# Attention and routed experts on one core: queries and keys projected with channels on the partitions, expert choice and first loads moved ahead, zeros written in the attention stage

## The reference

```
xn = layernorm(x)                       # x: 16 x 1024 x 256, float32
q, k, v = xn @ W_q, xn @ W_k, xn @ W_v  # split into 16 heads of 16 channels
q, k = rope(q), rope(k)                 # x * cos + [-x2, x1] * sin over each head's 16 channels
attn = softmax(causal(q @ k.T) / sqrt(16))
s = concat(attn @ v) @ W_o
logits = xn @ w_router.T                # 8 experts; every token goes to its argmax
h = leaky(xn @ w_fc[e].T, 0.5) ** 2     # only the chosen expert's output is kept
out = x + s * silu(h @ w_proj[e].T)
```

## Time and profile before

| | |
|---|---|
| median of 3 runs | 2603.72 us (2599.06 to 2605.83) |
| the profiled execution | 2609.07 us, its span 2607.3 us |
| PE, DVE, ACT, POOL busy, share of the span | 95%, 81%, 68%, 38% |
| project_phase | up to 428.7 us |
| attention_phase | 428.7 to about 2240 us |
| expert_output_phase | the rest |

### The profile page before, as it was taken

How to read it: one execution, slowest core, us unless ns; L and a number is a source line. 1 busy time by engine, 2 the same in 40 slices (tenths; PEclk the granted TensorE clock), 3 DMA queues, 4 the chain that set the end, 5 groups by cost and what they waited for, 6 DMA issues and landing times. The chain is left out here.

```text
span 2607.3 us, 53565 instructions
## 1 busy us (share of the span) xinstructions
PE 2484.7 (95%) x16876; PEld 1292.0 (50%) x16877; DVE 2110.2 (81%) x6183; ACT 1773.4 (68%) x4187; POOL 987.6 (38%) x1187
## 2 busy tenths in 40 slices
PE   7999993999999999999999999999999999899887
PEld 6888782334334334343343343343343343588776
DVE  7888886888889888899899888898888898355344
ACT  5777771577777777777777777777777777655211
POOL 7888885122222222222222222222222222222666
PEclk9999996899999999999999999999999999999898
DMA  7999997655646546546557556466465461498898
GB/s 241 356 346 355 353 340 205 124 93 106 116 99 109 113 91 114 116 93 117 103 99 150 104 101 118 93 104 118 99 108 115 91 110 48 139 308 303 271 349 258
DMA packets 305865, 435.04 MB, mean 167 GB/s; under 512 B 101808, under 2 KB 204464, under 8 KB 305584
## 3 DMA queue, kind: packets, MB, share of 16 engines
q1 hardware_dynamic: 293296, 398.05, 61.0%
q0 software_dynamic: 12288, 33.57, 4.7%
HBM read 241.18 MB, written 188.74 MB: 165 GB/s over the span
## 5 line engine op out<-in xcount | busy, mean ns | idle before, releaser
L866 ACT ACTIVATE probs<-ps_cols 128x512 f32<-128x512 f32 (+3 forms) x3072 | 1313.5, 498 | 478.9 <-PE ps_cols L1035 467.2
L887 DVE CUSTOM_DVE_ANT_0 dump<-ps_rows,mask 128x128 bf16<-128x128 f32 (+7 forms) x2048 | 1472.0, 754 | 199.2 <-issue 166.9
L1035 PE MATMUL ps_cols<-q_st,k_st 99*128 99x512 bf16 (+3 forms) x3072 | 857.6, 329 | 5.5 <-DMA q_st<-max_T 3.2
L845 POOL TENSOR_SCALAR_AFFINE_SELECT probs<-probs 128x512 f32<-128x512 f32 x512 | 324.6, 634 | 1321.3 <-ACT probs L866 1321.3
L979 PE MATMUL ps_rows<-k_st,q_st 96*128 96x512 bf16 (+3 forms) x3072 | 768.8, 330 | 27.2 <-DMA v_st<-v_dram 21.9
L1011 PE MATMUL ps_ctx<-probs,v_st 128*32 128x512 f32 (+3 forms) x6144 | 642.0, 497 | 1.6 <-ACT ctx_raw L858 0.8
L1035 PEld LDWEIGHTS ps_cols<-q_st,k_st 99*128 99x128 bf16 x3072 | 273.4, 97 | 595.0 <-ACT probs L866 390.1
L979 PEld LDWEIGHTS ps_rows<-k_st,q_st 96*128 96x128 bf16 x3072 | 277.5, 98 | 292.4 <-DVE row_max L887 130.4
L1011 PEld LDWEIGHTS ps_ctx<-probs,v_st 128*32 128x32 f32 x6144 | 129.3, 108 | 188.7 <-issue 113.5
L280 POOL TENSOR_TENSOR roped<-rope_c,rope_s 128x512 f32<-128x512 f32 x128 | 164.8, 1287 | 40.7 <-DVE rope_s L404 40.7
L887 DVE DVE_READ_ACCUMULATOR2_ANT row_max<- 128x1 f32 x2048 | 170.0, 83 | 0.2
(11 more groups left out here) (113 smaller groups left out, 2613.3 us busy)
## 6 DMA issues: line engine op xcount, KB each, us to landing
parts_dram<-parts SPq DMA_DIRECT2D x128, 384.0 KB, 3.9
q_st<-parts_dram SPq DMA_DIRECT2D x384, 128.0 KB, 4.4
k_st<-parts_dram SPq DMA_DIRECT2D x384, 128.0 KB, 6.9
v_dram<-v_sb SPq DMA_DIRECT2D x128, 256.0 KB, 5.5
v_st<-v_dram SPq DMA_DIRECT2D x64, 512.0 KB, 9.0
xs_dram<-zeros SPq DMA_DIRECT2D x36, 512.0 KB, 6.9
xs_sb<-xs_dram SPq DMA_DIRECT2D x72, 256.0 KB, 4.8
g_dram<-g_sb SPq DMA_DIRECT2D x72, 256.0 KB, 3.9
```

The costliest lines, as they stand in the source:

```text
L845: nc.gpsimd.affine_select(out=tri, in_=tri, compare_op=ALU.is_ge, fill=0.0, base=0, pattern=[[0, GH], [1, P]], channel_multiplier=-1).then ...
L866: nc.scalar.activation(probs[:, k % PB, h, 0:w], ps_cols[(GH * k + h) % CB][:, 0:w], ACT.Exp).then_inc(exp_done, 1)
L887: nc.vector.tensor_tensor_reduce(out=dump[:, even, 0:n], in0=ps_rows[:, 512 * bank:512 * bank + n], in1=mask[:, S - n:S], scale=1.0, scala ...
L1035: nc.tensor.matmul(ps_cols[(GH * k + h) % CB][:, 0:w], k_st[r][:, j // IB, h * 512 + (j % IB) * P:h * 512 + (j % IB + 1) * P], q_st[r][:, ...
```

## The change

- **Queries and keys are projected with channels on the partitions.** The weights are now the stationary operand and the turned tile the moving one (`heads` on PE). A unit `m` is one of 64: queries (`a` = 0) or keys (`a` = 1) of one tile. Its two banks hold the first and second half of every head's channels (`k` = 0, 1), so the swap of halves is a swap of banks. DVE makes four products of 128x512 per unit (`rotate`; for queries with the factor 1/4 in the same instruction), POOL combines them in two instructions of 128x512 (`turn`), and the result is already laid out as it is stored: PE's turn back is gone. The parts are cut per unit, 1024 columns at once, and `take_rest` reads `roped` in SBUF where it read `ps_m` in PSUM.
- **Normalisation half a tile sooner.** ACT applies the first two sub-tiles of tile `t + 2` at the end of tile `t`; DVE's statistics stand in one piece at the start of a tile.
- **Values** are stored in rows of 68 columns where they had 128: the heads lie 17 apart, and a head's matmul in attention still takes 32 columns, of which 17 are used.
- **Experts are chosen** (`choose`) after DVE's last `rotate` and before its last `take_rest`. The one-hot table is written in the order in which it lies in memory.
- **Constants** of the attention stage (mask, identities) are made in the first stage, whose start they follow; the first group's operands are loaded in tile 8 (`first_operands`, `load_operands`).
- **Zeros** are written in the attention stage, four pieces in each of the first nine groups; the 128 scatters follow in the other 55 groups, two or three each.

The diff, cut to its core:

```diff
+def load_operands(sp, parts_dram, v_dram, b, r, q, k, v, loaded):
+
+    for a, (dst, slots) in enumerate(((q, SLOT_Q), (k, SLOT_K))):
+        for slot, part in enumerate(slots):
+            src = parts_dram[:, a, part].rearrange("(b c) (d g h) t -> b g d c (h t)", c=TPB, g=NG, h=GH)[b, r]
+            sp.dma_start(dst[slot * HD:(slot + 1) * HD], src).then_inc(loaded, 16)
+    src = v_dram[:, r].rearrange("(b c) p n -> b p c n", c=TPB)[b]
+    sp.dma_start(v[:, 0:NB * V_ROW].rearrange("p (c n) -> p c n", c=TPB), src).then_inc(loaded, 16)
...
-            for i in range(CLEARS * t // NT, CLEARS * (t + 1) // NT):
-                clear_xs(i)
+            if t > 0:
+                store_parts(t - 1)
+            if t == FIRST_GROUP_AT:
+                for j in range(TPB):
+                    sp.wait_ge(v_stored[j % 2], 16 * (j // 2 + 1))
+                    sp.wait_ge(parts_stored[j % 2], 32 * (j // 2 + 1))
+                load_operands(sp, parts_dram, v_dram, 0, 0, *first_in)
             sp.wait_ge(v_ready, SUB * (t + 1))
-            for g in range(NG):
-                sp.dma_start(v_dram[t, g], v_sb[:, u, g]).then_inc(v_stored[u], 16)
-            sp.wait_ge(part3_done, SUB * (t + 1))
-            for blk in range(4):
-                sp.dma_start(parts_dram[t, blk].rearrange("a r t -> r a t"),
-                             parts[:, u, blk]).then_inc(parts_stored[u], 16)
+            sp.dma_start(v_dram[t].rearrange("g p n -> p g n"),
+                         v_sb[:, u].rearrange("p g s n -> p g (s n)")).then_inc(v_stored[u], 16)
+        store_parts(NT - 1)
         for u in range(2):
-            sp.wait_ge(v_stored[u], 16 * NG * NT // 2)
-            sp.wait_ge(parts_stored[u], 64 * NT // 2)
+            sp.wait_ge(v_stored[u], 16 * NT // 2)
+            sp.wait_ge(parts_stored[u], 32 * NT // 2)
             sp.wait_ge(xn_stored[u], 16 * NT // 2)
-        sp.wait_ge(xs_cleared, 16 * CLEARS)
...
+        def turn(m):
+
+            u = m % 2
+            pool.wait_ge(half_turned, m + 1)
+            if m >= 2:
+                pool.wait_ge(rest_ready, m - 1)
+            nc.gpsimd.tensor_tensor(roped[:, u, 0], rope_c[:, u, 0], rope_s[:, u, 0],
+                                    ALU.subtract).then_inc(roped_ready, 1)
+            pool.wait_ge(qk_used, 2 * m + 2)
+            nc.gpsimd.tensor_tensor(roped[:, u, 1], rope_c[:, u, 1], rope_s[:, u, 1],
+                                    ALU.add).then_inc(roped_ready, 1)
+
+        def part3(m):
+            t, a = divmod(m, 2)
+            pool.wait_ge(part2_done, m + 1)
+            nc.gpsimd.tensor_tensor(parts[:, t % 2, a, 2], rest[:, m % 2], parts[:, t % 2, a, 1],
                                     ALU.subtract).then_inc(part3_done, 1)
...
+        for m in range(NM + 2):
+            if m < NM:
+                turn(m)
+                if m % 2 == 0 and m // 2 + 2 < NT:
+                    scale(m // 2 + 2)
+            if m >= 2:
+                part3(m - 2)
...
+        def rotate(m):
+
+            t, a = divmod(m, 2)
+            u, at = m % 2, (t % TPB) * TOK
+            cos, sin = (rope_sb[:, i, at:at + TOK] for i in range(2))
+            first, second = ps_qk[2 * u], ps_qk[2 * u + 1]
+
+            def times(out, ps, table):
+                if a == 0:
+                    return nc.vector.scalar_tensor_tensor(out, ps[:], SCALE, table, ALU.mult, ALU.mult)
+                return nc.vector.tensor_tensor(out, ps[:], table, ALU.mult)
+
+            if m >= 2:
+                dve.wait_ge(roped_ready, 2 * (m - 1))
+            dve.wait_ge(qk_ready, 2 * m + 1)
+            times(rope_c[:, u, 0], first, cos)
+            times(rope_s[:, u, 1], first, sin).then_inc(qk_used, 1)
+            dve.wait_ge(qk_ready, 2 * m + 2)
+            times(rope_s[:, u, 0], second, sin).then_inc(half_turned, 1)
+            times(rope_c[:, u, 1], second, cos).then_inc(qk_used, 1)
+
+        def take_rest(m):
+            t, a = divmod(m, 2)
+            dve.wait_ge(part1_done, m + 1)
+            if m >= 2:
+                dve.wait_ge(part3_done, m - 1)
+            nc.vector.tensor_tensor(rest[:, m % 2], roped[:, m % 2].rearrange("p k t -> p (k t)"),
+                                    parts[:, t % 2, a, 0], ALU.subtract).then_inc(rest_ready, 1)
...
+        for m in range(NM + 1):
+            t, a = divmod(m, 2)
+            if m < NM:
+                if a == 0 and t + 2 < NT:
+                    ln_stats(t + 2)
+                    ln_scale(t + 2)
+                if a == 1 and t + 1 < NT:
                     xT_lo(t + 1)
...
+                rotate(m)
+            else:
+                choose()
+            if m >= 1:
+                take_rest(m - 1)
...
+        def heads(m, k):
+
+            t, a = divmod(m, 2)
+            cols = slice((2 * a + k) * P, (2 * a + k + 1) * P)
+            if m >= 2:
+                pe.wait_ge(qk_used, 2 * (m - 2) + k + 1)
+            three_passes(ps_qk[2 * (m % 2) + k][:], lambda i, c: w_all_hl[i][:, c, cols],
+                         lambda j, c: xT_hl[j][:, t % 2, c, :]).then_inc(qk_ready, 1)
...
+        for m in range(NM):
+            t, a = divmod(m, 2)
+            pe.wait_ge(xT_lo_ready, DC * (t + 1))
+            values(2 * m)
+            if a == 1 and t + 1 < NT:
+                transpose_xn(t + 1, (2, 3))
+            heads(m, 0)
+            values(2 * m + 1)
+            if a == 0 and t + 1 < NT:
+                transpose_xn(t + 1, (0, 1))
+            heads(m, 1)
...
-    SUBS_SCATTERED = NT * SUB // N
+    CLEARS = NBLK * BLK // (4 * P)
+    CLEAR_GROUPS = 9
+    CLEARED = CLEARS // CLEAR_GROUPS
+
+    def subs_scattered(n):
+
+        at = [NT * SUB * max(m - CLEAR_GROUPS, 0) // (N - CLEAR_GROUPS) for m in (n, n + 1)]
+        return range(*at)
...
+            if n < CLEAR_GROUPS:
+                for i in range(CLEARED // 2):
+                    clear_xs(CLEARED * n + i)
             store_ctx(n, b, r, 0)
             if not last:
                 load_max(n + 1, (r + 1) % RING, 0)
-            t = n // SUBS_SCATTERED + 1
-            if n % SUBS_SCATTERED == 0 and 2 <= t < NT:
-                sp.wait_ge(scattered[t % 2], 16 * SUB * (t // 2))
...
-                mm = nc.tensor.matmul(ps_ctx[VW * h:VW * (h + 1), o:o + w], v_st[r][:, j, VW * h:VW * (h + 1)],
+                mm = nc.tensor.matmul(ps_ctx[VW * h:VW * (h + 1), o:o + w], v_st[r][:, j * V_ROW + VP * h:j * V_ROW + VP * h + VW],
...
```

438 lines of the change are left out of this document (200 added, 238 removed).

## The result

| | before | after |
|---|---|---|
| median | 2602.52 us (2599.06 to 2605.83) | 2651.22 us (2650.50 to 2662.60) |
| profiled execution, its span | 2609.07, 2607.3 us | 2651.32, 2649.6 us |
| forecast for the median | | 2613, range 2564 to 2640 |

A forecast was written before the change was run, and what follows sets the result against it. The prediction took DMA to set the old tile period, PE half a microsecond behind. Its terms, 21.5 + 1 + 1.5 + 0 - 15.2 + 0.5, gave +9.3 us: 2613 us for the median, range 2564 to 2640.

The forecast's parts named there:

- tiles and the load in them: First stage: tile period 12.95 instead of 12.17 us, +21.5 us in all; loading group 0 in tile 8, +1.5.
- start: Before the tiles: weights cut in five instructions instead of one, on ACT and then DVE, 0 to 2 us, +1 taken.
- end of the stage: After the tiles: cheaper choice of experts against waits for POOL, 24.0 us against 24.3, counted as nothing.
- wait for group 0: Between first stage and row items: PE's wait while SP loads group 0's operands goes, -15.2 us.
- attention, first column scores to first expert block: Attention: zero pieces and a third scatter stay hidden behind PE, +0.5 us (0 to 3).
- the plain sums: Tiles: busy time per engine without exclusion, largest 10.3 us on POOL, giving a period of about 11.2 us.
- The price of 1.05 us on POOL: Tiles: what POOL pays for each subtraction when DVE is first, between 0 and 1.22 us, 1.05 taken.
- the barrier: Between first stage and attention: PE's first row item was to come within 1 us of it.
- the three rivals: Tiles: periods 11.2, 12.1 or 13.75 us, times 2554, 2585 or 2639; chances 0.16, 0.13, 0.16 (last with the clock).
- the gap: Tiles: once per tile POOL waits for DVE's statistics and three products, 0.2 to 0.6 us, 0.5 taken.
- the third rival: Tiles: POOL's next instruction gets ahead of waiting DVE; period 13.75, 2639 us; chance 0.16 together with the clock.
- the first rival: Tiles: the exclusion between DVE and POOL hardly counts; period 11.2 us, -50, 2554 us; chance 0.16.

The follow-up runs named there:

- e4: Changed kernel with DVE's subtraction split into two halves that read their first input from PSUM (stored parts not right): 2597.3 us, ratio 0.9975 to the kernel before.
- e2: Changed kernel with DVE running the statistics behind the four products instead of ahead of them in even units: 2605.09 us, ratio 1.0011 to the kernel before.
- e1: Changed kernel with the two small operations at the end of the statistics made by POOL instead of DVE: 2630.93 us, ratio 1.0106 to the kernel before.
- e5: Kernel before with only the zeros moved from the tiles into the first nine groups of attention: ratio 0.9973 to the kernel before.
- e11: e10 with ACT's copies and DVE's subtractions of the next tile's transposed x one sub-tile sooner: ratio 0.9930 to the kernel before.
- e12: e11 with the statistics of the tile after next also closed one sub-tile sooner: 2648.27 us, ratio 0.9875 to the kernel before on that chip.
- e6: Changed kernel with the projection loop of the kernel before, all other parts of the change kept: ratio 0.9937 to the kernel before.
- e7: Changed kernel with group 0 loaded by the attention stage, as before, instead of in tile 8: ratio 1.0184 to the kernel before.
- e9: e2 with the 13 loads of group 0 spread over tiles 8 to 20 instead of all in tile 8: ratio 0.9981 to the kernel before.
- e10: e6 with the 13 loads of group 0 spread over tiles 8 to 20: median 2582.9 us, ratio 0.9915 to the kernel before.
- the first four experiments: Changed kernel with small operations on POOL, statistics behind the products, both, or the subtraction reading PSUM: 2630.93, 2605.09, 2623.35, 2597.3 us.

## Why the prediction was wrong

By its own terms, in the profiled executions:

| term | forecast | measured |
|---|---|---|
| tiles and the load in them | +21.5 + 1.5 | +64.3 |
| start | +1 | +0.9 |
| end of the stage | 0 | -0.1 (24.34 to 24.26) |
| wait for group 0 | -15.2 | -15.2 |
| row items | 0 | +1.7 (27.2 to 28.9) |
| attention, first column scores to first expert block | +0.5 | -2.3 |
| experts and output | 0 | -7.1 |
| sum | +9.3 | +42.3 |

The other 5 us of the miss in the median are the offset of 5.35 us between profile and median, which I applied to both kernels and which was 0.1 us in the kernel after.

**What held.** The mechanism I chose over the plain sums: an exclusion between DVE and POOL, on both sides, first come first served. The price of 1.05 us on POOL is 0.95 (e4). The subtraction, both turns and the third part came out within 0.15 us of the forecast, the one-hot took 1.22 us, the barrier went as said. None of the three rivals came true. e2's tile of 12.52 us is nearly the sum that I made for POOL, without the gap (12.45).

**The step that failed** is the gap: "from the subtraction into the statistics (2.9 less two `xT_lo` at 0.61, 1.7 us, up to 2.1 with their waits) and three products (1.8) before POOL may turn: 3.5 to 3.9 us, against 3.3 of POOL's own work". The work of POOL was 3.3 us, as forecast. DVE took 5.2 (205.58 to 210.75 us), since L427 in it took 1.53. That is 1.97 us of idle POOL per tile instead of 0.5, and 1.36 of the 1.47 between them are the hold of L427 (1.53 less 0.17). 1.47 x 30 tiles with statistics are 44 us: the tiles missed the forecast by 41. I had applied the exclusion to the 1024 columns alone, as "a DVE instruction with both inputs in SBUF", and took the small operations at the length that they had before. But in the kernel before L364 always ran as POOL came to its end: in 30 of 32 tiles it started 0.12 or 0.13 us before the end of POOL's sum, in the first two with nothing on POOL. The row for it was not wrong, it had no wait to show. Other rows had. The prediction names L433, one input, SBUF to SBUF, which took 0.26 us and ended 0.03 us after POOL's third part, and it drew on this row against the third rival, but wrote all the same that instructions without two inputs in SBUF don't wait. And in attention the first small operation on the row maxima takes 0.28 to 0.31 us in 57 of 128 cases, each time beside a scatter on POOL, and 0.17 in nearly all others:

```profile
L900 DVE TENSOR_SCALAR max_parts<-row_max x128: 169/171/314, 452.7 to 2221.3; 128x16 bf16<-128x16 f32 x128
```

The Trainium skill had it, on the page and in the section that the prediction cites ("SBUF — State Buffer", "Who interferes with whom"): besides the two-input form it counts copies, casts and `tensor_scalar` among the operations that can contend for the shared port pair, when their operands meet the conditions of a two-port mode. I read the half sentence on two inputs and left the one on one input. The trace agrees, with 1.43 us for L427, and with 1.88 us for L970 beside a mere fill on POOL. e1 shows that it was this operation, e2 that its place decides what it costs.

**A second error, without effect on the sum:** "So DMA sets the period, with PE half a microsecond behind." e5 refutes it. PE was busy for 95.6% of the tiles (first line) and waited once a tile in the ring that e11 and e12 show. That 4.26 MB at 350 GB/s gave just 12.2 us was a circle: the 350 GB/s are the bytes of a tile over its time. It did mislead two expectations, e5's and e6's. The "1.9 by which DVE's and POOL's periods exceed their work" is also off: by its own numbers it is 1.6 for POOL and 1.8 for DVE, which touches the first rival's period alone.

**Smaller ones.** The load in tile 8 costs 4.3 to 4.6 us, not 1.5 (e7, e9), and 9.1 in the old loop (e6, e10). The prediction counted 2.1 MB for it with the values at their old width; with rows of 68 columns it is 1.8. PE's granted clock in the tiles fell from 1.00 to 0.87, a mix of its two levels, 1.00 and 0.50 in turn; PE stood 93.9 us for DVE's `xT_lo` there, and DVE's products waited 4.0 us for PE (16 to 440 us), so this set nothing. I had looked for a fall to the lower level only. The row items are 1.7 us longer, with L970 and L977 held; in e7, where the fills run ahead of them, they take 27.2 us as before. The expert stage, whose work the change leaves alone, took 344.3 us where it took 351.4; in the first four experiments, on one chip, it took 341.4 to 352.4, so I read nothing in it. What makes it so wide is open.
